# A graph layer on one Trainium2 core: in TensorE's round, the sums of a couple ahead of the product by W2

## What is computed

```
h = relu(layernorm(x))
e = concat(h[src], h[dst])                    # one row for each edge
m = relu(e @ W1 + b1) @ W2 + b2               # 128 hidden values, 64 out
s, cnt = segment_sum(m, dst), segment_sum(1, dst)
out = x + s / max(cnt, 1)
```

## Time and profile before

| | |
|---|---|
| device time, median of 3 runs | 1985.01 us (1983.43 to 1985.71) |
| the profiled execution, its own time | 1985.82 us |
| its span, first to last instruction | 1983.9 us |
| TensorE busy | 1263.6 us (64%) |
| VectorE busy | 866.6 us (44%) |
| ScalarE busy | 280.0 us (14%) |
| GpSimd busy | 1479.1 us (75%) |
| mean granted clock of TensorE | 0.832 of full |

### The profile page before, as it was taken

One profiled execution on the slowest core, in us unless ns is written; L12 is line 12 of the kernel. 1 busy time (PEld: TensorE's weight loads), 2 busy tenths in 40 slices (PEclk: granted clock), 3 DMA queues, 4 the chain that ended last, 5 costly groups with the idle time before them and its releaser, 6 DMA issues.

```text
span 1983.9 us, 20481 instructions
## 1 busy us (share of the span) xinstructions
PE 1263.6 (64%) x7608; PEld 1072.6 (54%) x7609; DVE 866.6 (44%) x1571; ACT 280.0 (14%) x429; POOL 1479.1 (75%) x1572
## 2 busy tenths in 40 slices
PE   5879665665555666666656666656666666666666
PEld 4769554555555545555545555555555555555554
DVE  9688433333333334343443433443333344444444
ACT  3232111111111111111111111111111111111111
POOL 6777777777777777777777777777777777777774
PEclk9889878777878778888888888888887877887887
DMA  8744323232323232333223333333232334333332
GB/s 180 226 142 124 89 78 88 77 89 77 89 77 92 80 92 80 93 90 91 80 83 89 84 89 91 92 81 92 80 102 80 96 84 111 85 101 85 110 85 50
DMA packets 122381, 188.67 MB, mean 95 GB/s; under 512 B 32449, under 2 KB 83944, under 8 KB 122276
## 3 DMA queue, kind: packets, MB, share of 16 engines
q0 software_dynamic: 50016, 101.22, 19.7%
q1 hardware_dynamic: 71695, 85.86, 14.4%
q10 hardware_dynamic: 564, 0.23, 0.1%
HBM read 170.59 MB, written 16.59 MB: 94 GB/s over the span
## 4 chain that ended last, share of the span: by engine, by line
POOL 70%; issue 23%; PE 3%; DVE 2%; DMA 1%; ACT 0%; ACTq 0%; POOLq 0%; DVEq 0%
POOL g L489 70%; DMA g<-p_table,src_e 1%; PE bank L1054 1%; DVE rows_b L684 1%; PE z L1041 1%; DVE stats L668 0%; POOL g L470 0%; DVE work L806 0%; PE bank L1072 0%; PE bank L937 0%; PE bank L1061 0%; DVE acc L834 0%; PE z L937 0%; DVE g L824 0%; PE bank L1082 0%
## 5 line engine op out<-in xcount | busy, mean ns | idle before, releaser
L489 POOL DMA_INDIRECT g<-p_table,src_e x1523 | 1438.9, 945 | 464.2 <-issue 462.4
L824 DVE TENSOR_TENSOR g<-z,g 128x1024 f32<-128x1024 f32 x196 | 239.2, 1220 | 1059.9 <-DMA g<-p_table,src_e 1058.4
L1041 PE MATMUL z<-work 128*128 128x128 f32 x1568 | 292.1, 363 | 316.8 <-DVE work L806 316.2
L1041 PE MATMUL z<-w,work 128*128 128x128 f32 x1558 | 290.8, 363 | 303.5 <-DVE work L806 302.9
L1041 PEld LDWEIGHTS z<-work 128*128 128x128 f32 x1568 | 269.4, 268 | 333.5 <-DVE work L806 333.4
L1041 PEld LDWEIGHTS z<-w,work 128*128 128x128 f32 x1558 | 267.1, 267 | 320.4 <-DVE work L806 319.8
L601 ACT ACTIVATE g<-g 128x1024 f32<-128x1024 f32 x196 | 206.6, 1054 | 1608.8 <-DVE g L824 1608.8
L1054 PE MATMUL bank<-work,g 128*128 128x128 f32 x3126 | 415.4, 288 | 0.0
L1054 PEld LDWEIGHTS bank<-work,g 128*128 128x128 f32 x3126 | 382.4, 200 | 46.5 <-issue 46.5
L813 DVE TENSOR_TENSOR work<-bank,rel_e 128x1024 f32<-128x1024 f32 x196 | 238.8, 1218 | 6.5 <-PE bank L1054 3.9
L806 DVE TENSOR_SCALAR_CACHE_REDUCE work<-rel_q,rows_f 128x1024 f32<-128x1024 bf16 (+1 forms) x116 | 126.7, 1104 | 1.6 <-DMA rel_q<-rel_table 1.6
(11 more groups left out here) (97 smaller groups left out, 320.1 us busy)
## 6 DMA issues: line engine op xcount, KB each, us to landing
rel_q<-rel_table SPq DMA_DIRECT2D x49, 512.0 KB, 4.0
rows_b<-rel_table SPq DMA_DIRECT2D x49, 512.0 KB
g<-p_table,src_e POOLq DMA_INDIRECT x1523, 2.5
work<-q_table SPq DMA_DIRECT2D x100, 64.0 KB
w<-q_table SPq DMA_DIRECT2D x99, 64.0 KB
p_table<-g SPq DMA_DIRECT2D x12, 448.0 KB
q_table<-work SPq DMA_DIRECT2D x12, 448.0 KB
out_dram<-xs SPq DMA_DIRECT2D x5, 448.0 KB
```

The source lines that it names most:

```text
L489: nc.gpsimd.indirect_dma_start(out=g[:, slot(n), j * HID:(j + 1) * HID], out_offset=None, in_=p_table, in_offset=bass.IndirectOffsetOnAxis ...
L824: nc.vector.tensor_tensor(rows_of_p(m), z_all[m % 2][:, 0:HID * chunks_in(m)], rows_of_p(m), ALU.add)\
L1041: last = nc.tensor.matmul(z_all[m % 2][:, at:at + HID], spreads[m % 2][:, at:at + 128], qw[i % WINDOWS], start=True, stop=True)
```

## The change

In TensorE's `fast`, `sum_edges(m - 1)` moves ahead of `times_w2` of the block that ended two couples back. Both still come after `spread_q(m + 1)` and before `turn_sums`. The waits are inside the functions and go with them. No other engine's program changes.

```
                     if m + 1 < COUPLES:
                         spread_q(m + 1)
+                    if 1 <= m <= COUPLES:
+                        sum_edges(m - 1)
                     if 2 <= m < COUPLES + 2 and m - 2 == BLOCK_END[BLOCK[m - 2]]:
                         times_w2(BLOCK[m - 2])
-                    if 1 <= m <= COUPLES:
-                        sum_edges(m - 1)
                     for b in range(BATCHES):
                         if MEAN_AT[b] == m:
```

## The result

| | before | changed |
|---|---|---|
| median of 19 runs each | 1985.35 us (1982.24 to 1987.06) | 1988.25 us (1986.01 to 1990.23) |
| span of the profiled execution | 1983.9 us | 1986.4 us |
| granted clock of TensorE, mean | 0.832 | 0.818 |

The ratio is 1.0017, 95% interval 1.0011 to 1.0023, which is 2.2 to 4.6 us. The forecast was 1986.1 us in 1983.4 to 1988.8, with 0.93 for a change under 0.2%. The direction is right; the size of 1.1 us is too small.

The account below looks back on a forecast made before the run. GpSimd's gathers, one per 1.25 us, were taken to bound the kernel until the last gather. Terms 0 + 0 + 0 + 1.1 us on the median 1985.01 gave 1986.1 us, range 1983.4 to 1988.8.

Parts of the forecast that it names:

- (a): Earlier `u_psum`: GpSimd's waits gain 1.1 to 2.1 us but hold no gather; worth 0, ceiling 1.8 us.
- (b): Later `v_psum` in the catch-up: block at most 10.6 us, catch-up ends at most 30 us later, cost 0.
- VectorE's wait for L1054 at L813: Sign in 120 to 205 us, the catch-up: this wait for the sums was to be gone.
- (c): Later `v_psum` in steady rounds: product at most 1.0 us late, covered by VectorE's 6.38 us of idle time; cost 0.
- My ring for that experiment: Half the gathers, new order: one turn of add, spreads, sums and product at full clock, 6.6 to 6.8 us.
- The 230 us forecast from it: Half the gathers: 1.6 us for each of 96 one-group couples from 64 on, 2.2 us for each of 35 two-group ones.
- (d): The end, without cover: turn of batch 23 comes 1.15 us later, the end moves by +1.1 us.
- my upper bound of 2.4: The end moves by +2.4 us if the first step's sums and product are wholly slow, 3.78 and 2.06 us.
- one whole product more on the path: In the end, a product on the path beside the sums' slower start; their early start gives 1.6 us back.
- R1: Rival: neutral end, 1984.8 to 1985.0 us, sums of 194 find the clock up; chance 0.17.
- the sum had 0.2: The end moves by -0.2 us if the sums of 194 run wholly at 2.4 GHz.
- R3: Rival, slower: ring of add, spreads, sums, product, 7.6 to 12.0 us, bounds above 10.0 us; up to 70 us; chance 0.05.

Follow-up runs that it names:

- `e1_tail_only`: New order only in TensorE's rounds from 194 on, old order before, against the kernel before: 1984.63 us, ratio 1.0001.
- `e4_early_add`: Kernel before, TensorE's order kept; from round 193 VectorE adds sums ahead of rows, ScalarE copies 193's sums before 194's relu: 1981.58 us, ratio 0.9988.
- `e8_busy_end`: Changed kernel plus 12 idle products at the end of round 194, on the slower chip: 2511.82 us, ratio 1.0258 to the kernel before.
- `e8b_busy_end`: Changed kernel plus 12 idle products at the end of round 194, where the kernel before takes 1987.77 us: 1988.64 us, ratio 1.0003.
- `e5b_early_add_new_rounds`: `e4_early_add` with TensorE's new order in rounds 0 to 192, on a chip like the first: 1982.48 us, ratio 0.9991 to the kernel before.
- `e2_all_but_tail`: New order in TensorE's rounds 0 to 193, old order from 194 on, against the kernel before: 1982.46 us, ratio 0.9996.

## Why the prediction was right, and where it was short

- (a) Earlier sums release no gather: right. Gaps of 0.30 us before and after, and a lead of 36 quads releases none.
- (b) The catch-up: a block 9.97 us (at most 10.6 forecast), first landing waited for 27.4 us later (up to 30), no gather held. In the other profiles with the new order in the rounds it came at 215 to 238 us (199 to 204 us with the old), so "at most 30" was too tight. One sign did not come true: VectorE's wait for L1054 at L813 in 120 to 205 us was to be gone and is 3.8 us, where it was 3.9.
- (c) The steady rounds: the product ends in time, 2.4 us ahead of its add in the round shown. That the cover is real, and large when gone, is shown by half the gathers: 281 us. My ring for that experiment, 6.6 to 6.8 us, was between the 6.2 and 7.8 measured. The 230 us forecast from it was too small in two places: the couples 64 to 159 cost 186 us, where 96 times 1.6 is 154, and the 19 us before couple 64 had no price. The rounds with two groups came at 76 us, as forecast.
- (d) The end: each step in the order named, with the add of 194 bare. Forecast 1.15 us, measured 1.46 us in the profiled execution. The mis-sized term is the sums of 194: 3.66 us, where I took 3.4 on the ground that the clock would rise at the same moment as before. The all-slow 3.78 us occurred in three of the other profiles, and `e1_tail_only`, with the product slow too, lost 2.56 us to the kernel before, just over my upper bound of 2.4. The idle time ahead of the sums was 4.92 us, where the kernel before has 2.12 us ahead of its product: 2.4 us of the difference come from round 194, whose spread, sums and product ran at the full clock in 3.83 us instead of 6.23, and 0.4 us from the product that had moved. The prediction also spoke of one whole product more on the path. The chain before had it too, only ahead of the sums; what the order adds at a given clock is the later start (0.40 us) and the bare add (0.87 us). The Trainium skill, page "TensorE: Matmul & The Clock Gate", Part 1, has the throttled clock as the default that activity lifts. By that rule the sums take 3.78 us behind the idle time; the trace agrees (3.66, and 2.05 once idle products ran ahead of them), but in `e4_early_add` they took 2.05 us behind 2.65 us of idle time.
- The whole: 2.2 to 4.6 us by the 19 runs, while the end explains 1.46 in the profile, or 1.2 as the difference of the mean turns (9.34 of three new, 8.10 of two old). The 1.0 us of pace between the two profiles would bring it to 2.5 us, but that it belongs to the order is not shown. At least 0.7 us of the measured difference is thus unplaced; the medians of the partial kernels, each 2 us uncertain either way, don't find it.
- R1 (neutral end) needed sums at the full clock, and with idle work that is what came: 0.18 us under the 7.42 us, where the sum had 0.2. R3 had 0.05. On chips like the first no such loss came; on the slower chip the rounds lost 63 to 65 us. I had given R3 its price and its condition, a ring over 10.0 us, but taken for granted that TensorE's speed is that of the one trace.

## What to carry to other kernels

An exchange of two blocks on one in-order engine moves two events, one earlier and one later; ask of each who waits, and of the later one whether it closes a ring with the engine that feeds this one. Cover hides the ring only while the bound engine's round is longer: gathers of 10.0 us a couple hid it, gathers of 5.0 us did not (6.2 to 7.8 us a turn), and neither did the 10.0 us on a chip on which TensorE was late and a turn took 11.5 us. Compare two orders at the same clock: the new end with a full clock (7.24 us) looks as good as the old one with a partly low clock (7.42 us), and is not. In a kernel held by one engine for 96% of its time, the place to earn found here is the end: let what is ready long before (here adds and copies of older blocks) run ahead of the last landing, and keep TensorE at work before the matmuls that count (1.64 us shorter in the one end that was read).

## What the runs showed of the hardware that was not expected

- The pace of the same gathers differs from profile to profile: 1.2481 to 1.2507 us from gather to gather, even through the kernel, which is 4 us over 1523 of them; it is as large as the effect studied. The first of them starts between 61.5 and 65.4 us in the eight profiles of chips like the first, which is as much again. The time from the last mean to the end of the span also came in two groups, 2.5 to 2.7 us and 3.7 to 4.3 us, on the same code (2.65 us in `e8_busy_end`, 3.65 us in `e8b_busy_end`).
- One chip ran the kernel before at 2446 us in place of 1985, with the gathers still at 0.95 us each and VectorE's instructions as long as ever, but TensorE late and with 327 to 350 us of idle time put down to issue.
- The last sixteen sums took 3.66 to 3.78 us behind 3.3 to 5.0 us of idle time and 2.05 us behind 2.9 us of products that nobody reads. Between the two the length of the idle time did not tell: 2.65 us were followed by sums at the full clock (2.05 us, `e4_early_add`), 2.70 us by sums of 2.57 us (`e5b_early_add_new_rounds`), 2.80 us by a product and sums that were slow (3.71 us, `e2_all_but_tail`).
